# One of four attention row tiles normalised on VectorE instead of GpSimd

## The reference, cut to what matters

```
h = tok(x)                                        # 8 batches x 512 tokens x 256
att = q @ k.T / 8 + slope[head] * (i - j)         # 16 heads, causal, 512 x 512
m = max(att);  e = exp(att - m)
att = e / (1 + sum(e));   out = (att @ v) @ Wo
h = h + attention(layernorm(h));  h = h + ffn(layernorm(h))
```

## Time and profile before

| | us |
|---|---|
| median of 3 runs | 953.24 |
| lowest, highest | 951.85, 954.5 |
| the profiled execution, its device time | 954.45 |
| its span, first to last instruction | 952.6 |
| mean granted TensorE clock | 0.977 of full |

### The profile page before, as it was taken

The page is one execution under the profiler, slowest core; times in us unless marked ns, Lnnn a source line. Parts: engine busy times, 40 slices in busy tenths (PEclk is TensorE's granted clock), DMA queues, the critical chain, the costliest instruction groups (busy, mean ns, idle before and its releaser), DMA issues.

```text
span 952.6 us, 16893 instructions
## 1 busy us (share of the span) xinstructions
PE 865.0 (91%) x5552; PEld 670.9 (70%) x5552; DVE 607.5 (64%) x1898; ACT 728.7 (76%) x1611; POOL 629.7 (66%) x599
## 2 busy tenths in 40 slices
PE   7999668999999998999899999999999989999976
PEld 6888646767866786578667866787667866787663
DVE  4565636776685658575847684767676775668421
ACT  6855248998788868986889688977887798869813
POOL 6000068899686877687768877787859786768620
PEclk9999868999999999999999999999999999999997
DMA  9333350001000200020001100010001000000000
GB/s 268 63 111 111 126 184 1 1 2 56 2 1 1 78 1 1 1 79 1 1 1 45 35 1 1 23 57 1 1 23 56 2 1 23 1 2 1 10 14 22
DMA packets 23605, 33.55 MB, mean 35 GB/s; under 512 B 2608, under 2 KB 20176, under 8 KB 23520
## 3 DMA queue, kind: packets, MB, share of 16 engines
q1 hardware_dynamic: 19760, 19.01, 6.3%
q0 software_dynamic: 3760, 13.48, 5.0%
HBM read 17.80 MB, written 14.68 MB: 34 GB/s over the span
## 4 chain that ended last, share of the span: by engine, by line
PE 41%; DVE 13%; POOL 13%; ACT 10%; issue 10%; DMA 0%; DVEq 0%; POOLq 0%; ACTq 0%
PE ps L1039 11%; POOL probs L751 10%; PE ps L1173 9%; PE ps L1157 5%; DVE probs L921 5%; PE ps L1145 4%; PE ps L1125 4%; ACT probs L785 4%; PE ps L1146 3%; ACT turned_sb L792 3%; POOL token_rows L739 3%; DVE o_lo L973 2%; PE ps L1119 1%; ACT q_both L802 1%; DVE xn L910 1%
## 5 line engine op out<-in xcount | busy, mean ns | idle before, releaser
L751 POOL TENSOR_SCALAR probs<-probs,sums 128x512 f32<-128x512 f32 (+3 forms) x512 | 545.2, 1081 | 159.8 <-DVE sums L930 159.4
L921 DVE CUSTOM_DVE_ANT_0 probs<-ps,causal,slope 128x512 f32<-128x512 f32 (+3 forms) x512 | 260.2, 547 | 135.4 <-PE ps L1146 133.7
L785 ACT ACTIVATE probs<-probs,least 128x512 f32<-128x512 f32 (+3 forms) x512 | 284.4, 557 | 37.7 <-DVE least L921 31.1
L792 ACT ACTIVATE turned_sb<-ps 128x1280 f32<-128x1280 f32 x128 | 157.4, 1229 | 59.3 <-PE ps L1157 59.2
L1145 PE MATMUL ps<-k_hi,q_both 128*128 128x512 f32 (+3 forms) x512 | 183.1, 358 | 20.5 <-DVE least L921 18.3
L1157 PE MATMUL ps<-ident,probs 128*128 128x128 f32 x1280 | 162.0, 274 | 5.5 <-POOL probs L751 5.5
L1173 PE MATMUL ps<-turned_sb,token_rows 128*64 128x512 f32 (+3 forms) x1024 | 152.0, 438 | 13.4 <-ACT turned_sb L792 13.4
L1146 PE MATMUL ps<-k_lo,q_both 128*128 128x512 f32 (+3 forms) x512 | 153.4, 325 | 0.0
L1157 PEld LDWEIGHTS ps<-ident,probs 128*128 128x128 f32 x1280 | 143.6, 141 | 6.9 <-POOL probs L751 6.7
L1173 PEld LDWEIGHTS ps<-turned_sb,token_rows 128*64 128x64 f32 x1024 | 74.9, 136 | 98.7 <-issue 81.8
L1145 PEld LDWEIGHTS ps<-k_hi,q_both 128*128 128x128 f32 x512 | 97.1, 190 | 65.2 <-DVE least L921 39.3
(11 more groups left out here) (194 smaller groups left out, 1426.0 us busy)
## 6 DMA issues: line engine op xcount, KB each, us to landing
out_dram<-token_rows SPq DMA_DIRECT2D x7, 512.0 KB, 2.9
token_table<-made SPq DMA_DIRECT2D x4, 768.0 KB, 4.0
rows<-in_L_tok_codebook_dram SPq DMA_DIRECT2D x4, 512.0 KB, 9.0
w_f<-in_L_tok_W_dram SPq DMA_DIRECT2D x8, 256.0 KB, 6.3
early_rows<-made SPq DMA_DIRECT2D x4, 512.0 KB, 2.9
early_values<-xn SPq DMA_DIRECT2D x4, 512.0 KB, 3.0
token_table<-xn SPq DMA_DIRECT2D x4, 512.0 KB, 4.3
wo_f<-in_L_attn_Wo_dram POOLq DMA_DIRECT2D x1, 1024.0 KB, 9.8
```

Source lines behind the costliest of these rows:

```text
L751: ins = pool.tensor_scalar(at, at, recip[:, s % P_RING, q:q + 1], None, ALU.mult)
L785: act.activation(at, at, ACT.Exp, bias=least[:, s % P_RING, q:q + 1], scale=-1.0, accum_out=sums[:, s % P_RING, q:q + 1]).then_inc(exped, 1)
L792: act.activation(turned_sb[:, s % 2, :], turn_ps, ACT.Copy).then_inc(moved, 1)
L921: dve.tensor_tensor_reduce(out=probs[:, s % P_RING, at], in0=bank(unit % 2)[:, UNIT_AT[q]:UNIT_AT[q] + P * (q + 1)], in1=causal[:, at], sc ...
```

## The change

`normalize` on POOL leaves out tile 0, the one of 128 columns, and goes through tiles 3, 2, 1. DVE gets `normalize_first`, one `tensor_scalar` of 128x128 on that tile with a semaphore of its own, `first_normed`. It stands in slot s behind `least_of(s, 0)` and works on head s - 1. `turn` on PE waits for both semaphores.

```diff
@@ normalize (POOL)
                 pool.wait_ge(recip_done, s + 1)
-                for q in Q_ORDER:
+                for q in (3, 2, 1):
                     at = probs[:, s % P_RING, Q_AT[q]:Q_AT[q] + P * (q + 1)]
@@ normalize_first (DVE)
+            def normalize_first(s):
+
+                at = probs[:, s % P_RING, Q_AT[0]:Q_AT[0] + P]
+                dve.wait_ge(recip_done, s + 1)
+                dve.tensor_scalar(at, at, recip[:, s % P_RING, 0:1], None, ALU.mult).then_inc(first_normed, 1)
@@ loop of DVE
                 if s < ALL:
                     least_of(s, 0)
+                if 1 <= s <= ALL:
+                    normalize_first(s - 1)
+                if s < ALL:
                     least_of(s, 1)
                     least_of(s, 2)
@@ turn (PE)
                 pe.wait_ge(normed, s + 1)
+                pe.wait_ge(first_normed, s + 1)
```

More of the change, by code:

```diff
@@ L663, in layer @@
                                                  sem("normed"))
+    first_normed = sem("first_normed")
     turned, moved, valued = sem("turned"), sem("moved"), sem("valued")
```

## The result

Seven runs of each kernel: 950.0 us (949.24 to 951.1) against 953.64 (951.85 to 954.5). The ratio is 0.9966, 95% interval 0.9955 to 0.9977. The first rival, with 948.7, came nearest. The profiled execution took 949.98 us, its span 948.2 against 952.6.

A forecast was written before the change was run, and what follows sets the result against it. PE was taken to bound the kernel, so what counts is where it idles. The terms 3.5 + 2.1 + 0.6 - 5.5 gave +0.7 us, 953.9 against the median of 953.24, with a range of 948.7 to 960.

The forecast's parts named there:

- Rival 1: DVE hides nearly all of the new multiply's cost and only the gain is left: 948.7 us; chance 0.2.
- What bounds the kernel: PE, busy 865.0 of 952.6 us, is the engine to watch; it seldom waits for POOL, longer for DVE.
- The gain: PE's wait for POOL at the turn behind the gathers, 0.95 us in six batches, goes entirely: 5.5 us.
- The price of one multiply: x, DVE's delay per head: 0.33 us with the bare minimum read-out, plus 0.07 for POOL's holds, 0.40 in all.
- The norm stage: Layer norm, DVE without a gap: two multiplies cost 0.8, L903 gives back 0.3; net 0.5, seven batches: 3.5 us.
- The product u: PE's product u starts 0.3 us late behind DVE's y_lo, seven times: 2.1 us.
- Where x is hidden: Even slots: DVE idles 0.81 us; k-projection slots: it waits 0.56 for k_hi; output-product slots: PE is the bound.
- The first batch: Slots with no projection: the 384-column tile's minimum comes 0.15 to 0.2 us late, three times: 0.6 us.
- The second semaphore: PE's extra wait in turn: between 0 and 0.05 us each, 0 to 6 in all; taken as 0.
- Rival 2: Norm stage, slot of pos_lo: POOL's 384-column piece holds the multiply about 0.35 us; +6.7, 959.9 us; chance 0.25.
- Rival 3: POOL's multiply blocks DVE for its whole length: about +40, 993 us; chance 0.03.

The follow-up runs named there:

- e5: The changed kernel with the new DVE multiply one place earlier, ahead of the slot's first minimum: 954.12 us, ratio 0.9998.
- e6: The changed kernel with the 256-column tile moved to DVE as well: 963.9 us, ratio 1.0105.
- e1: The kernel before with POOL leaving out tile 0, which nobody multiplies: 942.57 us, ratio 0.9883.
- e2: The kernel before, POOL multiplying all four tiles, plus a DVE 128x128 multiply of a constant tile into an unused one, PE waiting for it: 958.11 us, ratio 1.0052.
- e3: The changed kernel with DVE multiplying tile 0 only for heads 0 and 1 of batches 1 to 6: 947.32 us, ratio 0.9942.
- e4: The kernel before with the four gathers of a batch issued in slot 4 instead of slot 1: 945.63 us, ratio 0.9916.
- e7: The changed kernel with the gathers in slot 4 instead of slot 1: 949.91 us, ratio 0.9959.
- e10: The kernel before with one more 128x384 multiply on POOL just ahead of the gathers, slot 1 of batches 1 to 6: 967.13 us, ratio 1.0144.
- e9: e4 with POOL taking the tiles in the order 3, 2, 1, 0 instead of 3, 2, 0, 1: 948.21 us, ratio 0.995.

## Why the prediction was wrong, step by step

**What bounds the kernel** was right: POOL's busy time is no measure, one wait per batch is, and it is at the turn of head 1.

**The gain** (5.5 us, "all of the row") was the right place and mis-sized: it measured 1.15 to 1.16 a batch, 6.9 us in all, in five of the seven kernels of the table that have no wait there; e5 and e6 show more, behind a loss in the slots just ahead. The row gives the idle time behind the modelled end of the last matmul, but matmuls overlap: the next one would have started 0.12 us behind the start of the last, 0.16 before its end. And the first transposes after a wait take 0.05 us longer together (1.31 against 1.26).

**The price of one multiply**, x = 0.40, was the step that failed, and with it the norm stage, for which the forecast has a net loss. It measured 0.20 in most slots and 0.23 by the mean. Two of its parts were wrong. The read-out of the minimum does not lie bare: the multiply starts together with it, as the next tile did (both at 555.40, with the tile behind them at 555.60). And a scalar less than L374 makes it 283 ns, not 341. So 0.20 and not 0.33; the lower bound of 0.25 was above the truth. The addition for being held, 0.07, is 0.03 by the mean.

**The norm stage** (+0.5 a batch, 3.5 us) became -0.2. Two multiplies cost 0.4 less a slack of about 0.1: the two slots behind 553.70 took 9.68 us before, and after the change 9.70 although L928 was 0.24 shorter. Against them L903 gave 0.23, nearly the 0.3 foreseen, and L928 at 562.76 gave 0.24 that I hadn't counted. The halves show where this comes from: L928 takes 0.34 to 0.35 there with POOL's half alone (e1) and 0.35 to 0.36 with DVE's half alone (e2). So about half of it comes with POOL's shorter head and half with DVE's own later arrival. PE's wait for xn got shorter. The forecast that it would grow was wrong.

**The product u** (+0.3) measured +0.20, by x, and there were two more such places that the forecast had at nothing: the slot ahead (+0.19, where q_lo, o_lo and y_lo follow each other) and that of the burst (+0.17). Together 0.59 a batch. The single steps: the forecast had 0.8 a batch for the norm stage and u, the changed kernel shows 0.39.

**Where x is hidden** held: the k_hi gap went from 0.56 to 0.36, and in e3, e4 and e7 the output-product slots carried every gain to the end of the batch.

**The first batch** (+0.6 in all) lost 0.2, but not at the slots named: from its fourth head on the shift changes by -0.1 us. **The second semaphore** for PE, put at nothing, costs nothing that shows: the turn gains 1.15 us with it and 1.16 without it (e1).

**Rival 2** (the held multiply in the slot of pos_lo) did not come: 0.28 us there, at 550.47. Held multiplies do exist, up to 794 ns, but in slots 3, 4 and 0 of the batches, where the delay doesn't reach PE: with the same multiplies and POOL unrelieved (e2), the stretches that hold these slots change by 0.02 us or less. **Rival 3** fell: half of the multiplies began in the middle of a POOL piece of 1.56 us and took 0.28 to 0.30 us. **Rival 1** was the right one, with nearly all of x hidden or repaid. I gave it 0.2 because the price of x was twice too high. With x = 0.20 the same sum gives 0.7 + 0.7 - 5.5 = -4.1, that is 949.1 (949.5 on the later median of 953.64). That this lies so near 950.0 is in part luck: it lacks the two other places (+2.4 us) and L928 (-1.7), and has the turn 1.4 too small.

**The sum as it is**, term by term, with the shifts of all batches in the profiled executions:

| term, us | forecast | measured |
|---|---|---|
| turn behind the gathers | -5.5 | -6.9 |
| norm stage | +3.5 | -1.3 |
| product u | +2.1 | +1.4 |
| the slots of y_lo and of the burst | 0 | +2.4 |
| first batch | +0.6 | +0.2 |
| sum | +0.7 | -4.2 |

953.6 - 4.2 = 949.4; measured 950.0.

## What POOL does to a small DVE operation

The 128 multiplies fall at different phases of POOL's pieces (the profile's spans on POOL are rough). In the changed kernel:

- 64 begin 0.47 to 0.9 us into a piece of 1.56 us. They take 0.28 to 0.30 us and end half a microsecond or more ahead of the piece's end.
- 21 begin 0.03 us ahead of the end of a piece and take 0.28 us; it is POOL's next piece, of 384 columns, that takes 1.31 us where its mean is 1.25.
- Three begin 0.42 us into a piece that follows another without a gap: 0.34 us.
- The six of slot 3 begin 0.16 to 0.20 us into a 384-column piece that follows another: 0.48 to 0.50 us. The six of slot 4 begin 0.20 us into a 256-column one: 0.79 us, until 0.08 us behind its end. Six of slot 0 begin 1.02 us into a piece of 1.56 us: 0.61 to 0.63 us, until 0.1 us behind its end.
- The other 22 begin beside no multiply of POOL.

One that isn't held, with POOL's row (it begins 0.53 us into the first of the row's three pieces), then those of slots 3 and 4:

```profile
565.36 3.68 POOL L752 TENSOR_SCALAR probs<-probs,sums 128x512 f32<-128x512 f32 x3 [2.02 <-DVE sums L931]
565.89 0.28 DVE L937 TENSOR_SCALAR probs<-probs,sums 128x128 f32<-128x128 f32 x1
523.12 0.49 DVE L937 TENSOR_SCALAR probs<-probs,sums 128x128 f32<-128x128 f32 x1
528.05 0.79 DVE L937 TENSOR_SCALAR probs<-probs,sums 128x128 f32<-128x128 f32 x1
```

So a POOL piece does not hold DVE for its whole length. The Trainium skill (SBUF — State Buffer, the section on the two separate sides) has the loser blocked for the whole instruction, for a DVE operation in a two-port mode; no row here names the mode of this multiply. The first 64 don't bear the rule out: blocked so, each would have waited 0.6 us or more. The twelve of slots 4 and 0, which end just behind the end of their piece, look like it; what sets them apart is open. With every multiply blocked, the changed kernel would have been near 993 by the estimate of the third rival; it was 950.0. And L928's longest went from 517 to 816 ns, in slot 3, which PE leads, without cost.

## What to carry to other kernels

Before moving work off an engine, list the waits for it: 72.6 us off POOL was worth 6.9 at one wait per batch and some 2.5 where POOL had held up small operations of DVE (e1), and moving four gathers three slots on (945.6 and 947.0 us, faster than both kernels) was worth 7 to 8 with no work moved. Count the delay of an added instruction by start to start of its neighbours, and a wait of PE by start to start as well, since both overlap their ends. And count on the receiving side only the stretches that it leads: 0.20 us by 128 heads is 26 us, and 2.7 were paid.

## What was not expected of the hardware

In e10 PE waited 2.03 to 2.15 us at the turn of six batches. In three of them the granted clock then fell to the lower level (for some 3.4 us in the first of them, as worked out above), which cost 1.5 to 1.6 us more than the wait itself; such a wait and what followed it cost about 3.8 us. The waits of 0.95 us in the kernel before were not followed by it. In e9 it happened once, behind one of seven waits for xn of about 1.17 us. What tells the waits that were followed by it from those that weren't is open.
